# Edge counts from 16 buckets with one product per block, in a graph attention and mixture-of-experts kernel

## The chip, the cores and the metric

One core of one Trainium2 chip runs the whole program. The metric is the device time of one execution in microseconds; lower is better.

## The reference, cut to what matters

Two layers on 1024 nodes with 512 features. The first is a graph attention in which a pair of nodes counts only where an edge joins them, then a mixture of 8 experts (2 chosen per token); the second sums the rows of the neighbours, edge by edge, and then has an 8-head attention and a second mixture.

```python
src = concatenate([_s, _d, arange(1024)])        # 8192 + 8192 + 1024 = 17408 edges
dst = concatenate([_d, _s, arange(1024)])
# layer 0
q, k, v = x @ Wq + bq, x @ Wk + bk, x @ Wv + bv
adj = zeros((N, N)).at[src, dst].set(1.0)
a = q @ k.T / sqrt(512)
a = a * adj + (1.0 - adj) * -1e6
attn = softmax(a, axis=-1) @ v
# layer 1
neigh = segment_sum(feat[src], dst, num_segments=N)
rst = (1.0 + eps[0]) * feat + neigh
```

The kernel needs the matrix of edge counts C[src, dst], 1024 x 1024: `min(C, 1)` is the mask of the first attention, and C itself multiplies the features in the second layer.

## The kernel before, in words

Five engines run hand-written instruction lists and meet at semaphores. Every large product is done in three passes (`three_pass`, line 324): each float operand is split into a high half (made by ScalarE, `copy`) and a low half (made by VectorE, `lo`), and hi x hi, hi x lo and lo x hi are added up in PSUM.

Order of the first part of the program:

1. VectorE sorts the edges (lines 1028 to 1064). Edges lie as 128 partitions x 136 columns (`EC`). Each edge gets its row tile (`src >> 7`, 8 tiles of 128 rows), a running count within the tile, and from two small products on TensorE (line 1610) a place, so that the edges of one tile fill blocks of 128 edges. There are `EDGE_BLOCKS` = 136 + 8 = 144 blocks.
2. TensorE transposes the normalised rows and makes the projections Q and K, eight steps `i` of 24 products (line 1630), then V, eight tiles `t` of 12 (line 1645), then the scores QK, eight tiles of 24 (line 1657). Between them it moves the edges to their places, in 34 groups of four columns of edges (`move_edges`, line 1615): each is eight small products of a lane one-hot (`edge_lanes`, VectorE, `lanes`, line 1077) and a step function (`edge_steps`, ScalarE, `steps`, line 672), added up in PSUM bank 7. Both operands have two buffers: group q of lanes can be written once group q - 2 is moved. A group of moves is placed after the odd `k` of a step.
3. VectorE reads bank 7, subtracts neighbours, and so has for each block and lane the row and the column of its edge (`block_rc`). It builds the row masks (`count_rows`, line 1117), one 128 x 128 per block, the block's tile number (`block_tile`), and adds the values' bias to X.
4. The count loop (lines 1129 and 1678) runs in two rounds, one for each half of the 1024 columns. In a round each of 144 blocks needs a column mask (128 x 512, `lane's column == column number`) and one product, row mask x column mask, added to the PSUM bank of the block's tile (eight tiles, eight banks; the bank comes from a register). Seven of eight column masks are built by VectorE, the eighth by ScalarE as relu(1 - |column - c|). The masks have a ring of 8 groups of four. After a round the eight banks are copied to `CT`, half of them by ScalarE and half by VectorE.
5. The first attention (lines 1189 and 1723) takes tile after tile: mask and maximum on VectorE, exponential on ScalarE, transposes on TensorE, high and low halves, products with V.

SP issues the loads in a fixed order and stores the counts after the second round; GpSimd is idle until the attention's last mask. Two short quotes show the order of the lanes against the moves. On VectorE:

```python
        lanes()
        for i in range(1, 2 * KT):
            projected(i)
            lanes()
            lanes()
```

and on TensorE, in projection `i`:

```python
                if k == KT - 1:
                    got.then_inc(Q0["ps"], 1)
                if i >= 2 and k % 2:
                    move_edges()
```

`projected(i)` makes the low half of projection i, after ScalarE's high half, and the low half of a weight slot.

Of the kernel before, what the change touches and what calls it, by code (L numbers as in the profile page):

```python
# [16 lines left out]
F32 = mybir.dt.float32  # L17
# [16 lines left out]
def build(nc, a, out, ctx):  # L34
# [22 lines left out]
    assert EC % 4 == 0 and HB == 2 and GB == 8 and NT == 8 and KT == 4  # L57
# [52 lines left out]
    edge_lane = edge_const("edge_lane", [EC], F32, 1728)  # L110
    edge_step = edge_const("edge_step", [EC], F32, 2272)
    block_rc = edge_const("block_rc", [2, EDGE_BLOCKS], F32, 0)
    block_f = edge_const("block_f", [EDGE_BLOCKS], F32, 1152)
    minus_column = edge_const("minus_column", [EDGE_BLOCKS], F32, 1728)
    block_tile = edge_const("block_tile", [EDGE_BLOCKS], I32, 2816)
    tile_blocks, tile_end, tile_base = (edge_const(n, [NT], F32, 3392 + 32 * k) for k, n in enumerate(("tile_blocks", "tile_end", "tile_base")))
    tile_i = edge_const("tile_i", [NT], I32, 3488)
    tile_count16 = edge_const("tile_count16", [NT], F16, 3520)
# [61 lines left out]
    in_tile = arena("in_tile", [P, NT, EC], F32, 118)  # L180
    seen_in = arena("seen_in", [P, 1 + NT * EC], F32, 122.5)
    tile_past = arena("tile_past", [P, EDGE_BLOCKS, NT], F32, 128)
# [4 lines left out]
    late_columns = arena("late_columns", [P, RING - 2, 4, HALF], F16, 64)  # L187
    act_columns = arena("act_columns", [P, 4, HALF], F16, 88)
    distance = arena("distance", [P, 2, HALF], F16, 92)
# [83 lines left out]
    act_columned, distanced = sem("act_columned"), sem("distanced")  # L273
    counted_act, counted_dve = sem("counted_act"), sem("counted_dve")
# [63 lines left out]
    def _(sp):  # L338
# [73 lines left out]
        wait(columns_used, 2 * COUNT_GROUPS)  # L412
        for t in range(NT):
            wait((counted_act, counted_dve)[t % 2], NT // 2 + t // 2 + 1)
            sp.dma_start(counts_d[t * P:(t + 1) * P, :], CT[:, t, :]).then_inc(A["stored"], 16)
# [14 lines left out]
        wait(Q0["bias"], 1)  # L430
# [72 lines left out]
    def _(gp):  # L503
# [78 lines left out]

        wait(A["m2"], NT)
# [55 lines left out]
    def _(act):  # L639
# [32 lines left out]
        def steps():  # L672
            q = stepped[0]
            stepped[0] += 1
            if q == 0:
                act.wait_ge(sort_dve, SORTS[1])
            if q >= 2:
                act.wait_ge(edges_moved, q - 1)
            for j in range(4):
                got = act.activation(edge_steps[:, q % 2, j, 0:STEPS_OF], blocks16[:, :], ACT.Sign,  # L680
                                     bias=edge_step[:, 4 * q + j:4 * q + j + 1])
            got.then_inc(edges_stepped, 1)

        for i in range(2 * KT):
# [6 lines left out]
            if i:  # L691
                steps()
            steps()
# [5 lines left out]
        for t in range(NT):  # L699
            act.wait_ge(Q0["s_ps"], t + 1)  # L700
            copy(SR[:, t, :], banks((4, 0)[t % 2]), Q0["s_done"], scale=-D ** -0.5)
            for _ in range(min(2, QUADS - stepped[0])):
                steps()
        assert stepped[0] == QUADS

        per_round = COUNT_GROUPS // 2

        def column_distance(i):

            r, b = i // per_round, 8 * (i % per_round) + 7  # L710
            if i >= 2:
                act.wait_ge(act_columned, i - 1)
            act.activation(distance[:, i % 2, :], columns16[:, r * HALF:(r + 1) * HALF], ACT.Abs,
                           bias=minus_column[:, b:b + 1]).then_inc(distanced, 1)

        def column(i):
            if i >= 4:
                act.wait_ge(columns_used, 2 * (i - 4) + 2)
            act.wait_ge(distanced, i + 1)
            act.activation(act_columns[:, i % 4, :], distance[:, i % 2, :], ACT.Relu, bias=1.0, scale=-1.0).then_inc(act_columned, 1)  # L720

        def counts_out(r):
            act.wait_ge(columns_used, COUNT_GROUPS * (r + 1))
            for t in range(0, NT, 2):
                copy(CT[:, t, r * HALF:(r + 1) * HALF], PS[:, t, :], counted_act)

        act.wait_ge(sort_dve, SORTS[1] + 3)
        column_distance(0)
        for i in range(2 * per_round):
            if i + 1 < 2 * per_round:  # L730
                column_distance(i + 1)
            column(i)
            if i == per_round + 1:
                counts_out(0)
        counts_out(1)

        def no_edge(half, par):
            t = 2 * half + par
            act.wait_ge((counted_act, counted_dve)[par], NT // 2 + half + 1)
# [23 lines left out]
        no_edge(0, 0)  # L763
        no_edge(0, 1)
# [208 lines left out]
    def _(v):  # L973
# [48 lines left out]
        def sort(ins):  # L1022
# [7 lines left out]
        per_tile = [P, NT, EC]  # L1030
        sort(v.tensor_scalar(tile_of[:, :], src_i[:, :], 7, None, ALU.logical_shift_right))
        sort(v.tensor_copy(tile_f[:, :], tile_of[:, :]))
        sort(v.tensor_tensor(in_tile[:, :, :], tile_f[:, :].unsqueeze(1).to_broadcast(per_tile),
                             blocks16[:, 0:NT].unsqueeze(2).to_broadcast(per_tile), ALU.is_equal))
        in_flat = in_tile[:, :, :].rearrange("p t c -> p (t c)")
        sort(v.tensor_tensor_scan(seen_in[:, 1:1 + NT * EC], in_flat, in_flat, 0.0, ALU.add, ALU.max))
        seen_before = seen_in[:, 0:NT * EC].rearrange("p (t c) -> p t c", t=NT)
        seen = seen_in[:, 1:1 + NT * EC].rearrange("p (t c) -> p t c", t=NT)
        v.tensor_tensor(tile_count16[:, :], seen[:, :, EC - 1], seen_before[:, :, 0], ALU.subtract).then_inc(sort_dve, 1)
        sorts[0] += 1  # L1040
        COUNTED = sorts[0]
        assert COUNTED == SORTS[0]

# [9 lines left out]
        v.wait_ge(sort_ps, 1)  # L1053
        tile_rank, tile_total = PS[:, 6, 0:NT], PS[:, 6, NT:2 * NT]
        sort(v.tensor_scalar(tile_i[:, :], tile_total, P - 1.0, None, ALU.add))
        sort(v.tensor_scalar(tile_i[:, :], tile_i[:, :], 7, None, ALU.logical_shift_right))
        sort(v.tensor_copy(tile_blocks[:, :], tile_i[:, :]))
        sort(v.tensor_tensor_scan(tile_end[:, :], ones16[:, 0:NT], tile_blocks[:, :], 0.0, ALU.mult, ALU.add))
        sort(v.tensor_tensor(tile_base[:, :], tile_end[:, :], tile_blocks[:, :], ALU.subtract))
        sort(v.scalar_tensor_tensor(out=tile_base[:, :], in0=tile_base[:, :], scalar=float(P), in1=tile_rank, op0=ALU.mult, op1=ALU.add))  # L1060
        sort(v.tensor_tensor(tile_base[:, :], tile_base[:, :], seen_before[:, :, 0], ALU.subtract))
        sort(v.tensor_tensor(seen, seen, tile_base[:, :].unsqueeze(2).to_broadcast(per_tile), ALU.add))
        sort(v.tensor_tensor(in_tile[:, :, :], in_tile[:, :, :], seen, ALU.mult))
        sort(v.tensor_reduce(out=place_f[:, :], in_=in_tile[:, :, :].rearrange("p t c -> p c t"), axis=X_AXIS, op=ALU.add))
# [26 lines left out]
        sort(v.tensor_scalar(place_i[:, :], place_f[:, :], -1.0, None, ALU.add))  # L1091
        sort(v.tensor_scalar(place_i[:, :], place_i[:, :], 7, None, ALU.logical_shift_right))
        sort(v.tensor_copy(edge_block[:, :], place_i[:, :]))
        sort(v.scalar_tensor_tensor(out=edge_lane[:, :], in0=edge_block[:, :], scalar=-float(P), in1=place_f[:, :], op0=ALU.mult, op1=ALU.add))
        sort(v.tensor_scalar(edge_vals[:, :, 0], src_i[:, :], 1.0, 0.5, ALU.add, ALU.mult))
        sort(v.scalar_tensor_tensor(out=edge_vals[:, :, 0], in0=tile_f[:, :], scalar=-0.5 * P, in1=edge_vals[:, :, 0], op0=ALU.mult, op1=ALU.add))
        sort(v.tensor_scalar(edge_vals[:, :, 1], dst_i[:, :], 0.5, None, ALU.mult))
        sort(v.tensor_scalar(edge_step[:, :], edge_block[:, :], -1.0, -0.5, ALU.mult, ALU.add))
        assert sorts[0] == SORTS[1], sorts
# [15 lines left out]
        sort(v.tensor_scalar(minus_column[:, :], block_rc[:, 1, :], -1.0, None, ALU.mult))  # L1115
# [4 lines left out]
        per_block = [P, EDGE_BLOCKS, NT]  # L1120
        sort(v.tensor_tensor(tile_past[:, :, :], tile_end[:, :].unsqueeze(1).to_broadcast(per_block),
                             blocks16[:, 0:EDGE_BLOCKS].unsqueeze(2).to_broadcast(per_block), ALU.is_le))
        sort(v.tensor_reduce(out=block_f[:, :], in_=tile_past[:, :, :], axis=X_AXIS, op=ALU.add))
        sort(v.tensor_scalar(block_tile[:, :], block_f[:, :], NT - 1.0, None, ALU.min))
# [945 lines left out]
```

## Time and profile before

| | us |
|---|---|
| median of 3 runs | 1089.34 (1089.09 to 1094.71) |
| the profiled execution, its own time | 1087.22 |
| its span, first to last instruction | 1085.4 |
| TensorE busy (matmuls) | 881.8 |
| VectorE busy | 757.5 |
| ScalarE busy | 507.2 |
| GpSimd busy | 357.7 |
| mean granted TensorE clock | 0.916 of 2.4 GHz |

The time of an execution is a little longer than its span, since it holds what lies around the first and the last instruction. Matmuls are pipelined, so TensorE's busy time is an upper view of its work. In the rows, L12 is line 12 of the kernel; `out<-in` names the tiles; a bracket at the end of a row says how long the engine had stood idle before it and what released it.

### The profile page before, as it was taken

How to read it: one execution, taken by the hardware profiler on the slowest of the kernel's cores; microseconds unless marked ns; L12 is line 12 of the kernel's file. 1: busy time of each engine (PE TensorE's matmuls, PEld its weight loads, DVE VectorE, ACT ScalarE, POOL GpSimd, SP SyncE). 2: the span in 40 equal slices, each digit the busy share in tenths (PEclk: the TensorE clock that was granted, in tenths of full speed). 3: DMA queues.
4: the chain of work that ended last, by engine and by line, in shares of the span. 5: the costliest groups of instructions: out<-in, count | busy, mean ns of one | idle time of the engine just before them, and what ended most of it. 6: DMA issues, size and time to landing. Idle time of an engine off the chain costs nothing.

```text
span 1085.4 us, 13783 instructions
## 1 busy us (share of the span) xinstructions
PE 881.8 (81%) x4522; PEld 674.3 (62%) x4522; DVE 757.5 (70%) x1550; ACT 507.2 (47%) x880; POOL 357.7 (33%) x236
## 2 busy tenths in 40 slices
PE   2999997888864999298898788999999987745990
PEld 2777773336743887077687676777777766534860
DVE  8878599886796443857122776778687877796638
ACT  3567517655652554132303046656565656643530
POOL 1000000000202553007321327686786666703520
PEclk9999999998995999589999889999999999966995
DMA  5010000007261444423111330010010050272432
GB/s 160 30 22 2 1 1 1 1 21 265 66 231 59 137 154 139 164 98 98 49 49 29 107 78 1 20 49 20 11 30 20 1 175 1 87 251 100 154 141 103
DMA packets 55523, 84.74 MB, mean 78 GB/s; under 512 B 8976, under 2 KB 31760, under 8 KB 54944
## 3 DMA queue, kind: packets, MB, share of 16 engines
q1 hardware_dynamic: 49376, 63.94, 18.7%
q0 software_dynamic: 6080, 19.93, 5.6%
q8 instruction: 39, 0.64, 0.2%
q14 instruction: 28, 0.23, 0.1%
HBM read 57.11 MB, written 22.54 MB: 73 GB/s over the span
## 4 chain that ended last, share of the span: by engine, by line
PE 57%; DVE 32%; ACT 4%; issue 3%; DMA 2%; POOL 1%; SPq 0%; DVEq 0%; ACTq 0%; POOLq 0%
PE PS L328 37%; DVE late_columns L1138 4%; DVE neg_max L1507 3%; PE PS L1934 3%; PE PS L1949 3%; DVE APL L976 3%; PE PS L1948 2%; PE PS L1923 2%; DVE count_rows L1118 2%; PE PS L1842 2%; PE PS L1623 2%; PE PS L1785 2%; DVE early_columns L1138 1%; DVE XN L1009 1%; DVE XN L1575 1%
## 5 line engine op out<-in xcount | busy, mean ns | idle before, releaser
L615 POOL TENSOR_SCALAR AP__201<-AP__201,rden 128x1024 f32<-128x1024 f32 x64 | 181.9, 2847 | 84.6 <-DVE rden L1512 83.9
L556 POOL TENSOR_TENSOR W1L<-W1R,W1H 128x1024 fp32r<-128x1024 f32 x8 | 18.9, 2390 | 292.0 <-DVE neg_max L1157 288.2
L647 ACT ACTIVATE APH<-PS 128x512 fp32r<-128x512 f32 x128 | 71.7, 597 | 68.7 <-PE PS L1934 44.1
L1507 DVE TENSOR_REDUCE neg_max<-PS 128x1 f32<-128x1024 f32 x64 | 78.2, 1222 | 34.8 <-PE PS L1923 34.0
L976 DVE TENSOR_TENSOR APL<-PS,APH 128x512 fp32r<-128x512 f32 x128 | 83.1, 680 | 24.8 <-ACT APH L647 24.6
L328 PE MATMUL PS<-XTH,WH 128*128 128x512 f32 x224 | 81.8, 412 | 4.5 <-DVE XTL L976 4.5
L1934 PE MATMUL PS<-ident,AP__201 128*128 128x128 f32 x512 | 70.7, 280 | 12.6 <-DVE APL L976 10.8
L328 PE MATMUL PS<-XTL,WH 128*128 128x512 f32 x224 | 78.4, 397 | 0.0
L328 PE MATMUL PS<-XTH,WL 128*128 128x512 f32 x224 | 78.1, 395 | 0.0
L1934 PEld LDWEIGHTS PS<-ident,AP__201 128*128 128x128 f32 x512 | 59.4, 143 | 28.8 <-issue 16.8
L547 POOL CAST WH<-RAW 128x512 fp32r<-128x512 f32 x30 | 23.4, 781 | 158.5 <-PE PS L328 93.5
L917 ACT ACTIVATE AP__201<-PS,neg_max 128x1024 f32<-128x1024 f32 x64 | 71.5, 1117 | 7.4 <-DVE neg_max L1507 6.7
L566 POOL DMA_INDIRECT BX<-normalised,gather_i x38 | 40.1, 1055 | 90.1 <-DVE scatter_i L1329 69.8
L1085 DVE SCALAR_TENSOR_TENSOR edge_lanes<-lanes,edge_lane,edge_vals 128x256 f16<-128x256 f16 x136 | 55.6, 480 | 8.2 <-PE PS L1623 8.2
L1949 PE MATMUL PS<-APH,AV 128*128 128x512 f32 x128 | 50.8, 397 | 11.1 <-DVE APL L976 11.1
L579 POOL DMA_INDIRECT expert_rows<-BY,scatter_i x38 | 37.4, 985 | 61.9 <-ACT BY L647 61.9
L1602 PE MATMUL PS<-ident,XN 128*128 128x128 f32 x128 | 28.3, 398 | 36.2 <-DVE XN L1009 15.7
L680 ACT ACTIVATE edge_steps<-blocks,edge_step 128x145 f16<-128x145 f16 x136 | 45.3, 408 | 20.7 <-PE PS L1623 17.1
L976 DVE TENSOR_TENSOR BHL<-PS,BHH 128x256 fp32r<-128x256 f32 x38 | 16.1, 425 | 51.2 <-ACT BHH L647 51.2
L1138 DVE TENSOR_SCALAR late_columns<-columns,block_rc 128x512 f16<-128x512 f16 x189 | 50.5, 355 | 0.0
L328 PEld LDWEIGHTS PS<-XTH,WH 128*128 128x128 f32 x224 | 42.2, 193 | 13.4 <-POOL WL L549 3.5
L1697 PE MATMUL PS<-late_columns,count_rows 128*128 128x512 f16 x189 | 46.8, 389 | 4.5 <-DVE late_columns L1138 2.5
(302 smaller groups left out, 2393.4 us busy)
## 6 DMA issues: line engine op xcount, KB each, us to landing
YT<-expert_rows SPq DMA_DIRECT2D x12, 512.0 KB, 6.8
counts<-CT SPq DMA_DIRECT2D x8, 512.0 KB, 4.9
W1R<-in_L_ffn_w SPq DMA_DIRECT2D x8, 512.0 KB, 3.9
W2R<-in_L_ffn_w SPq DMA_DIRECT2D x8, 512.0 KB, 5.6
normalised<-XN SPq DMA_DIRECT2D x2, 2048.0 KB, 8.7
CG<-counts SPq DMA_DIRECT2D x8, 512.0 KB, 3.4
RAW<-in_L_gnn_W SPq DMA_DIRECT2D x16, 256.0 KB, 2.8
W1R<-in_L_ffn_W SPq DMA_DIRECT2D x8, 512.0 KB, 8.7
```

What stands on the lines that cost most here:

```text
L328: got = pe.matmul(o, lhs, r, start=first and j == 0, stop=last and j == 2)
L615: gp.tensor_scalar(AP_[:, i % 4, :], AP_[:, i % 4, :], rden[:, i % 4:i % 4 + 1], None, ALU.mult).then_inc(B["norm"], 1)
L647: act.activation(dst, src, Copy, **kw).then_inc(s, 1)
L680: got = act.activation(edge_steps[:, q % 2, j, 0:STEPS_OF], blocks16[:, :], ACT.Sign, bias=edge_step[:, 4 * q + j:4 * q + j + 1])
L917: act.activation(AP_[:, i % 4, :], banks(2 * (i % 2)), ACT.Exp, bias=neg_max[:, i % 4:i % 4 + 1], accum_out=denom[:, i % 4:i % 4 + 1]).the ...
L976: v.tensor_tensor(dst, src, f(hi), ALU.subtract).then_inc(s, 1)
L1085: got = v.scalar_tensor_tensor(out=edge_lanes[:, q % 2, j, :, :], in0=lanes1[:, :].unsqueeze(1).to_broadcast([P, 2, P]), scalar=edge_lane[ ...
L1138: got = v.tensor_scalar(count_columns(k, j), columns16[:, r * HALF:(r + 1) * HALF], block_rc[:, 1, b:b + 1], None, ALU.is_equal)
L1507: v.tensor_reduce(out=neg_max[:, i % 4:i % 4 + 1], in_=banks(2 * (i % 2)), axis=X_AXIS, op=ALU.max, negate=True).then_inc(B["mx"], 1)
L1697: got = pe.matmul(PS[:, ds(held[b % 24]), :].rearrange("p a n -> p (a n)"), count_rows[:, b, :], moving, start=False, stop=False, skip_gro ...
L1934: got = pe.transpose(PS[:, 4 + half, k * P:(k + 1) * P], AP_[:, i % 4, c * P:(c + 1) * P], ident[:, :])
L1949: got = pe.matmul(PS[:, 6, :], AV[:, hp % 2, h, k, :], APH[:, k, :], start=k == 0, stop=k == NT - 1)
```

## The change

Edges are sorted into 16 buckets instead of 8: the row tile times two, plus the half of the columns that the edge's `dst` lies in. There are 136 + 16 = 152 blocks, and each block belongs to one bucket, so it needs one column mask (of 512 columns) and one product: 152 of each, in one round. VectorE makes all column masks, in a ring of 6 groups. Bucket k is summed in PSUM bank k % 8. Banks are handed over by engines that read bucket ends from memory: SP counts finished buckets (`bucket_done`), ScalarE copies a finished bank to `CT` and zeroes it (`bank_free`), GpSimd grants banks to pairs of groups (`banks_granted`), and TensorE waits for the grants. The block-to-bank table comes from a third small product in place of a comparison of all blocks with all tile ends. The operations of the sort are spread between the projections' low halves. The edge products begin in projection 4 in place of 2, and up to four stand in a score tile in place of two. The bias of the values is added tile by tile inside the attention, and the exponential's table is loaded ahead of it.

The core of the diff:

```diff
-    EDGE_BLOCKS = EC + NT
+    BUCKETS = 2 * NT
+    EDGE_BLOCKS = EC + BUCKETS
-    RING = 8
-    SORTS = (5, 23)
+    RING = 6
+    SORTS = (7, 18, 29)
...
     SP:
-        wait(columns_used, 2 * COUNT_GROUPS)
+        wait(sort_dve, PLACED)
+        for k in range(BUCKETS - 1):
+            last = sp.value_load(last_group[0:1, k:k + 1], min_val=1, max_val=COUNT_GROUPS)
+            wait(columns_used, last)
+            sp.sem_inc(bucket_done, 1)
+        wait(columns_used, COUNT_GROUPS)
...
     GpSimd:
+        for g in range(COUNT_GROUPS // 2):
+            needed = gp.value_load(banks_needed[0:1, g:g + 1], min_val=1, max_val=BUCKETS)
+            wait(bank_free, needed)
+            gp.sem_inc(banks_granted, 1)
...
     ScalarE, after the high half of projection i:
-            if i:
+            if i >= 4:
                 steps()
-            steps()
+            if i >= 3:
+                steps()
...
+        def count_out(k):
+
+            if k < BUCKETS - 1:
+                act.wait_ge(bucket_done, k + 1)
+            else:
+                act.wait_ge(columns_used, COUNT_GROUPS)
+            copy(CT[:, k // 2, k % 2 * HALF:(k % 2 + 1) * HALF], PS[:, k % 8, :], counted)
+            if k < 8:
+                act.wait_ge(counted, k + 1)
+                copy(PS[:, k, :], PS[:, k, :], bank_free, scale=0.0)
...
     VectorE:
-        lanes()
-        for i in range(1, 2 * KT):
+        bucket_bases()
+        projected(1)
+        places()
+        projected(2)
+        edge_columns()
+        projected(3)
+        lanes()
+        for i in range(4, 2 * KT):
             projected(i)
+            if i == 5:
+                banks_of_blocks()
             lanes()
             lanes()
...
-        for r in range(2):
-            for g in range(COUNT_GROUPS):
-                k = COUNT_GROUPS * r + g
-                for j in range(4 - g % 2):
...
+        for k in range(COUNT_GROUPS):
+            if k >= RING:
+                v.wait_ge(columns_used, k - RING + 1)
+            elif k == 2:
+                v.wait_ge(Q0["s_ps"], NT)
+            for j in range(4):
+                b = 4 * k + j
+                got = v.tensor_scalar(count_columns(k, j), columns16[:, 0:HALF], block_rc[:, 1, b:b + 1], None, ALU.is_equal)
+            got.then_inc(columns_ready, 1)
...
         mask(0, 0)
         mask(0, 1)
+        value_bias(0)
         p_lo(0, 0)
         for i in range(NT // 2 - 1):
             mask(i + 1, 0)
+            value_bias(2 * i + 1)
             p_lo(i, 1)
             residual(i, 0)
             mask(i + 1, 1)
+            value_bias(2 * i + 2)
             p_lo(i + 1, 0)
...
     TensorE, in projection i:
-                if i >= 2 and k % 2:
+                if i >= 4 and k % 2:
                     move_edges()
...
     TensorE, in score tile t:
-                if k % 2 and moved[0] < QUADS:
+                if moved[0] < QUADS:
                     move_edges()
...
+        for g in range(COUNT_GROUPS):
+            if g % 6 == 0:
+                n = min(24, EDGE_BLOCKS - 4 * g)
+                pe.load(tiles[0:n], block_bank[0:1, 4 * g:4 * g + n])
+                held = [pe.snap(q, min_val=0, max_val=7) for q in tiles[0:n]]
+            if g % 2 == 0:
+                pe.wait_ge(banks_granted, g // 2 + 1)
+            pe.wait_ge(columns_ready, g + 1)
+            for j in range(4):
+                b = 4 * g + j
+                got = pe.matmul(PS[:, ds(held[b % 24]), :].rearrange("p a n -> p (a n)"), count_rows[:, b, :],
+                                count_columns(g, j), start=False, stop=False, skip_group_check=True)
+            got.then_inc(columns_used, 1)
```

`bucket_bases`, `places`, `edge_columns` and `banks_of_blocks` hold the operations of the sort, now over 16 buckets: 11, 2, 9 and 6 of them.

## Rows read from the trace of the kernel before

**Rows 1.** The page, part 1: span, and busy time of TensorE.

```profile
span 1085.4 us, 13783 instructions
PE 881.8 (81%) x4522; PEld 674.3 (62%) x4522; DVE 757.5 (70%) x1550; ACT 507.2 (47%) x880; POOL 357.7 (33%) x236
```

**Rows 2.** Chain of waits, first 300 us: start, length, what.

```profile
135.93 23.53 DVE count_rows L1118 x144
...
168.81 5.51 DVE late_columns L1138 x21
```

**Rows 3.** Windows: stretch, length, busy time by engine, clock, DMA share, GB/s.

```profile
84.90:114.50 29.60, 29.60 (x216) 22.97 (x214) 28.52 (x67) 24.23 (x68) 0.00 (x0) 1.00 0.00 1
163.10:241.40 78.30, 69.67 (x304) 29.95 (x304) 72.51 (x258) 49.63 (x77) 0.00 (x0) 0.98 0.00 1
```

**Rows 4.** Timeline of VectorE in the sort: start, length, instruction, idle time before it.

```profile
5.67 2.43 DVE L1036 TENSOR_TENSOR_SCAN seen_in<-in_tile 128x1088 f32<-128x1088 f32 x1
...
28.98 1.29 DVE L1062 TENSOR_TENSOR seen_in<-seen_in,tile_base 128x1088 f32<-128x1088 f32 x1
...
31.64 2.25 DVE L1064 TENSOR_REDUCE place_f<-in_tile 128x136 f32<-128x1088 f32 x1
```

**Rows 5.** Timeline of all engines around a projection's end, 51 to 55 us.

```profile
51.66 1.11 ACT L688 ACTIVATE KH<-PS,bk 128x1024 fp32r<-128x1024 f32 x1 [1.47 <-PE PS L328]
...
52.80 1.28 DVE L979 SCALAR_TENSOR_TENSOR KL<-PS,bk,KH 128x1024 fp32r<-128x1024 f32 x1 [1.59 <-ACT KH L688]
...
54.60 3.25 DVE L1085 SCALAR_TENSOR_TENSOR edge_lanes<-lanes,edge_lane,edge_vals 128x256 f16<-128x256 f16 x8
```

**Rows 6.** Timeline of all engines in a value tile, 90 to 92 us.

```profile
90.56 0.60 ACT L647 ACTIVATE VH<-PS 128x512 fp32r<-128x512 f32 x1
...
91.19 0.69 DVE L976 TENSOR_TENSOR VL<-PS,VH 128x512 fp32r<-128x512 f32 x1
...
91.80 3.25 DVE L1085 SCALAR_TENSOR_TENSOR edge_lanes<-lanes,edge_lane,edge_vals 128x256 f16<-128x256 f16 x8
```

**Rows 7.** Timeline of TensorE at its waits.

```profile
81.49 0.79 PE L328 MATMUL PS<-WH,XTH 128*128 128x512 f32 x1 [2.59 <-DVE WL L976]
...
84.96 0.47 PE L328 MATMUL PS<-WH,XTH 128*128 128x512 f32 x1
...
86.92 0.48 PE L328 MATMUL PS<-WH,XTH 128*128 128x512 f32 x1
...
168.17 1.68 PE L1697 MATMUL PS<-early_columns,count_rows 128*128 128x512 f16 x7 [3.15 <-DVE early_columns L1138]
...
175.45 1.68 PE L1697 MATMUL PS<-late_columns,count_rows 128*128 128x512 f16 x7 [1.72 <-DVE early_columns L1138]
...
207.91 3.16 PE L1697 MATMUL PS<-late_columns,count_rows 128*128 128x512 f16 x7 [2.02 <-DVE late_columns L1138]
```

**Rows 8.** Windows of 3 us behind three of those waits.

```profile
81.50:84.50 3.00, 3.00 (x9) 2.09 (x10) 1.52 (x4) 0.00 (x0) 0.00 (x0) 0.50 0.02 5
168.20:171.20 3.00, 3.00 (x14) 1.41 (x15) 3.00 (x13) 2.14 (x4) 0.00 (x0) 1.00 0.00 0
208.00:211.00 3.00, 3.00 (x8) 1.12 (x9) 3.00 (x13) 0.17 (x1) 0.00 (x0) 0.50 0.00 0
```

**Rows 9.** Timeline from the last edge product to the first column mask.

```profile
134.67 0.46 DVE L1113 COPY block_sum<-PS 128x290 f32<-128x290 f32 x1 [5.02 <-PE PS L1623]
...
161.96 1.02 ACT L647 ACTIVATE SR<-PS 128x1024 f32<-128x1024 f32 x1 [4.41 <-PE PS L328]
...
162.42 4.43 DVE L1126 TENSOR_TENSOR X<-X,row 128x4096 f32<-128x4096 f32 x1
```

**Rows 10.** Timeline from the first mask of scores to the first value product.

```profile
243.78 1.22 DVE L1153 SCALAR_TENSOR_TENSOR SM<-CT,SR 128x1024 f32<-128x1024 f32 x1
...
252.52 0.50 PE L328 MATMUL PS<-VH,PTH 128*128 128x512 f32 x1 [0.55 <-DVE PTL L976]
```

More of the change, by code:

```diff
@@ L272, in build @@
     rows_ready, columns_ready, columns_used = sem("rows_ready"), sem("columns_ready"), sem("columns_used")
-    act_columned, distanced = sem("act_columned"), sem("distanced")
-    counted_act, counted_dve = sem("counted_act"), sem("counted_dve")
+    bank_free, banks_granted, bucket_done = sem("bank_free"), sem("banks_granted"), sem("bucket_done")
+    counted = sem("counted")
     raw_in = [sem(f"raw_in{s}") for s in range(4)]
@@ L409, in results @@
                                  y_d[c * N + 2 * g * P:c * N + (2 * g + 2) * P, :].rearrange("(t p) d -> p t d", p=P)).then_inc(M["y_in"][g], 16)
-        wait(columns_used, 2 * COUNT_GROUPS)
+        wait(sort_dve, PLACED)
[4 more added lines that the diff above has]
+        wait(columns_used, COUNT_GROUPS)
         for t in range(NT):
-            wait((counted_act, counted_dve)[t % 2], NT // 2 + t // 2 + 1)
+            wait(counted, 2 * t + 2)
             sp.dma_start(counts_d[t * P:(t + 1) * P, :], CT[:, t, :]).then_inc(A["stored"], 16)
@@ L429, in _ @@
         results(0)
-        wait(Q0["bias"], 1)
+        wait(Q0["bias"], NT)
         sp.dma_start(row0[:, :], a["L1_gnn_b2"].partition_broadcast(P)).then_inc(row0_in, 16)
@@ L699, in _ @@
         for t in range(NT):
+            for _ in range(min(4, QUADS - stepped[0])):
+                steps()
             act.wait_ge(Q0["s_ps"], t + 1)
             copy(SR[:, t, :], banks((4, 0)[t % 2]), Q0["s_done"], scale=-D ** -0.5)
-            for _ in range(min(2, QUADS - stepped[0])):
-                steps()
         assert stepped[0] == QUADS
[L706 to L735, printed above, removed]
+        def count_out(k):
[7 more added lines that the diff above has]
+                copy(PS[:, k, :], PS[:, k, :], bank_free, scale=0.0)
         def no_edge(half, par):
             t = 2 * half + par
-            act.wait_ge((counted_act, counted_dve)[par], NT // 2 + half + 1)
+            act.wait_ge(counted, 2 * t + 2)
             if t >= 2:
@@ L761, in w1_hi @@
             copy(W1H[which][:, e, :, :], W1R[:, e, :, :], M["w_hi"])
-        no_edge(0, 0)
-        no_edge(0, 1)
+        for k in range(BUCKETS):
+            count_out(k)
+            if k in (1, 3):
+                no_edge(0, k // 2)
+            if k == BUCKETS - 2:
+                act.activation(inv[:, 0:1], neg_col[:, 0:1], ACT.Exp, scale=-1.0)
         softmax(0, 0)
@@ L1060, in _ @@
[L1060 to L1064, printed above, removed]
+        in_flat = in_bucket[:, :, :].rearrange("p t c -> p (t c)")
@@ new lines, in _, with bucket_bases @@
+        sort(v.tensor_tensor_scan(seen_in[:, 1:1 + BUCKETS * EC], in_flat, in_flat, 0.0, ALU.add, ALU.max))
+        seen_before = seen_in[:, 0:BUCKETS * EC].rearrange("p (t c) -> p t c", t=BUCKETS)
+        seen = seen_in[:, 1:1 + BUCKETS * EC].rearrange("p (t c) -> p t c", t=BUCKETS)
+        sort(v.tensor_tensor(bucket_count16[:, :], seen[:, :, EC - 1], seen_before[:, :, 0], ALU.subtract))
+        assert sorts[0] == SORTS[0]
+        def bucket_bases():
+            v.wait_ge(sort_ps, 1)
+            rank, total = PS[:, 6, 0:BUCKETS], PS[:, 6, BUCKETS:2 * BUCKETS]
+            sort(v.tensor_scalar(bucket_i[:, :], total, P - 1.0, None, ALU.add))
+            sort(v.tensor_scalar(bucket_i[:, :], bucket_i[:, :], 7, None, ALU.logical_shift_right))
+            sort(v.tensor_scalar(bucket_blocks[:, :], bucket_i[:, :], 1.0, None, ALU.max))
+            sort(v.tensor_tensor_scan(bucket_end[:, :], ones16[:, 0:BUCKETS], bucket_blocks[:, :], 0.0, ALU.mult, ALU.add))
+            sort(v.tensor_tensor(bucket_base[:, :], bucket_end[:, :], bucket_blocks[:, :], ALU.subtract))
+            sort(v.scalar_tensor_tensor(out=bucket_base[:, :], in0=bucket_base[:, :], scalar=float(P), in1=rank, op0=ALU.mult, op1=ALU.add))
+            sort(v.tensor_tensor(bucket_base[:, :], bucket_base[:, :], seen_before[:, :, 0], ALU.subtract))
+            sort(v.tensor_tensor(seen, seen, bucket_base[:, :].unsqueeze(2).to_broadcast(per_bucket), ALU.add))
+            sort(v.tensor_tensor(end_mask[0:BUCKETS, :], bucket_end[0:BUCKETS, :], ident[0:BUCKETS, 0:BUCKETS], ALU.mult))
+            sort(v.tensor_reduce(out=end_col[0:BUCKETS, :], in_=end_mask[0:BUCKETS, :], axis=X_AXIS, op=ALU.add))
+            sort(v.tensor_scalar(past16[0:BUCKETS, :], blocks16[0:BUCKETS, 0:EDGE_BLOCKS], end_col[0:BUCKETS, :], None, ALU.is_ge))
+            assert sorts[0] == SORTS[1], sorts
@@ new lines, in places, with edge_columns @@
+        def places():
+            sort(v.tensor_tensor(in_bucket[:, :, :], in_bucket[:, :, :], seen, ALU.mult))
+            sort(v.tensor_reduce(out=place_f[:, :], in_=in_bucket[:, :, :].rearrange("p t c -> p c t"), axis=X_AXIS, op=ALU.add))
+        def edge_columns():
+            sort(v.tensor_scalar(place_i[:, :], place_f[:, :], -1.0, None, ALU.add))
+            sort(v.tensor_scalar(place_i[:, :], place_i[:, :], 7, None, ALU.logical_shift_right))
+            sort(v.tensor_copy(edge_block[:, :], place_i[:, :]))
+            sort(v.scalar_tensor_tensor(out=edge_lane[:, :], in0=edge_block[:, :], scalar=-float(P), in1=place_f[:, :], op0=ALU.mult, op1=ALU.add))
+            sort(v.tensor_scalar(edge_vals[:, :, 0], src_i[:, :], 1.0, 0.5, ALU.add, ALU.mult))
+            sort(v.scalar_tensor_tensor(out=edge_vals[:, :, 0], in0=tile_f[:, :], scalar=-0.5 * P, in1=edge_vals[:, :, 0], op0=ALU.mult, op1=ALU.add))
+            sort(v.tensor_scalar(dst_i[:, :], dst_i[:, :], HALF - 1, None, ALU.bitwise_and))
+            sort(v.tensor_scalar(edge_vals[:, :, 1], dst_i[:, :], 0.5, None, ALU.mult))
+            sort(v.tensor_scalar(edge_step[:, :], edge_block[:, :], -1.0, -0.5, ALU.mult, ALU.add))
+            assert sorts[0] == SORTS[2], sorts
@@ L1119, in _, with value_bias @@
         got.then_inc(rows_ready, 1)
[L1120 to L1124, printed above, removed]
-        v.wait_ge(row0_in, 16)
-        v.tensor_tensor(X[:, :, :], X[:, :, :], row0[:, :].unsqueeze(1).to_broadcast([P, NT, D]), ALU.add).then_inc(Q0["bias"], 1)
-        v.wait_ge(Q0["bias"], 1)
-        for r in range(2):
-            for g in range(COUNT_GROUPS):
-                k = COUNT_GROUPS * r + g
-                if k >= RING:
-                    v.wait_ge(columns_used, k - RING + 1)
-                elif k == 2:
-                    v.wait_ge(Q0["s_ps"], NT)
-                for j in range(4 - g % 2):
-                    b = 4 * g + j
-                    got = v.tensor_scalar(count_columns(k, j), columns16[:, r * HALF:(r + 1) * HALF],
-                                          block_rc[:, 1, b:b + 1], None, ALU.is_equal)
-                got.then_inc(columns_ready, 1)
-            v.wait_ge(columns_used, COUNT_GROUPS * (r + 1))
-            for t in range(1, NT, 2):
-                v.tensor_copy(CT[:, t, r * HALF:(r + 1) * HALF], PS[:, t, :]).then_inc(counted_dve, 1)
+        for k in range(COUNT_GROUPS):
[7 more added lines that the diff above has]
+            got.then_inc(columns_ready, 1)
+        v.wait_ge(row0_in, 16)
+        def value_bias(t):
+            v.tensor_tensor(X[:, t, :], X[:, t, :], row0[:, :], ALU.add).then_inc(Q0["bias"], 1)
         def mask(half, par):
             t = 2 * half + par
-            v.wait_ge((counted_act, counted_dve)[par], NT // 2 + half + 1)
+            v.wait_ge(counted, 2 * t + 2)
             v.wait_ge(Q0["s_done"], NT)
@@ L1172, in residual @@
             v.wait_ge(A["rden"], t + 1)
+            v.wait_ge(Q0["bias"], t + 1)
             x = X[:, ds(t), :].rearrange("p a n -> p (a n)")
@@ L1608, in _ @@
         pe.wait_ge(setup, 12)
-        pe.wait_ge(sort_dve, SORTS[0])
-        pe.matmul(PS[:, 6, 0:NT], before16[:, :], tile_count16[:, :], start=True, stop=True)
-        pe.matmul(PS[:, 6, NT:2 * NT], ones16[:, :], tile_count16[:, :], start=True, stop=True).then_inc(sort_ps, 1)
         moved = [0]
@@ L1638, in _ @@
                     got.then_inc(Q0["ps"], 1)
-                if i >= 2 and k % 2:
+                if i >= 4 and k % 2:
                     move_edges()
+            if i == 0:
+                pe.wait_ge(sort_dve, SORTS[0])
+                pe.matmul(PS[:, 6, 0:BUCKETS], before16[:, :], bucket_count16[:, :], start=True, stop=True)
+                pe.matmul(PS[:, 6, BUCKETS:2 * BUCKETS], ones16[:, :], bucket_count16[:, :], start=True, stop=True).then_inc(sort_ps, 1)
+            elif i == 3:
+                pe.wait_ge(sort_dve, SORTS[1])
+                pe.matmul(PS[:, 6, 2 * BUCKETS:2 * BUCKETS + EDGE_BLOCKS], ones16[0:BUCKETS, :], past16[0:BUCKETS, :],
+                          start=True, stop=True).then_inc(sort_ps, 1)
         pe.wait_ge(w_ready, 12)
@@ L1721, in values @@
             got.then_inc(A["av_ps"], 1)
-        pe.wait_ge(counted_act, NT)
-        pe.wait_ge(counted_dve, NT)
+        pe.wait_ge(counted, BUCKETS)
         p_transposes(0, 0)
```

105 lines of the change are left out of this document (38 added, 67 removed).

## The prediction

> **What bounds the kernel now.** I read the page first: 1085.4 us of span, TensorE busy for 881.8 us of it [rows 1]. Next comes the chain of waits, cut to the first 300 us, because the change touches nothing later. It has two kinds of stretches. Where the projections run, it follows TensorE; from the last edge product on it follows VectorE, through 23.53 us of row masks and then the column masks [rows 2]. The windows say the same: while the values are projected TensorE is busy for 29.60 of 29.60 us, but VectorE for 28.52 as well; in the count loop TensorE is busy for 69.67 of 78.3 us and VectorE for 72.51 [rows 3]. So the count loop is paid in VectorE instructions, and the stage ahead of it has no slack on either engine. The change takes work out of the first and re-times the second.
>
> **The loop that gets shorter.** A block of edges now belongs to one bucket of (row tile, half of columns), so it needs one column mask and one product, where it had two. Before, VectorE made 252 masks and ScalarE 36; after, VectorE makes all 152. One costs 5.51 / 21 = 0.262 us on VectorE's path [rows 2]. After the last edge product VectorE copies sums (about 1 us) and makes 152 row masks at 23.53 / 144 = 0.163 us, 24.8 us; the two operations that compared blocks with tile ends and the 4.43 us bias addition [rows 9] are gone from there. In the new order half a score tile and five more follow the last edge product, 2.7 + 5 x 5.44 (4.41 + 1.03, the spacing of the score copies [rows 9]) = 29.9 us, so row masks and the first two groups of columns (8 x 0.262 = 2.1 us) hide behind them. The third group writes over the keys' low halves and waits for the end of the scores, which I call S (162.0 us before: the last copy starts at 161.96 [rows 9]).
>
> After S: 144 masks x 0.262 = 37.8 us on VectorE. TensorE waits 1.1 us for the last score copy, zeroes 8 banks (about 1.9 us) and then needs at most 4 x 1.68 / 7 = 0.96 us per group [rows 7] against VectorE's 1.05, so VectorE sets the pace. Then the mask of tile 0, its exponential, transposes, and high and low halves: before, 252.52 - 243.78 = 8.7 us [rows 10], 0.5 of it a table load that is now made early, so 8.3. First value product at S + 46.2; before, at S + 90.5 (252.52 - 162.0). **The loop gives 44.3 us back.**
>
> Work I cost at nothing: 16 copies of banks (0.6 us each) and 8 zeroings on ScalarE, some 15 us beside 38 us in which it has nothing else; the eight bias additions, 4.43 / 8 = 0.55 us each [rows 9], which lie where VectorE waits over 2 us for ScalarE's exponential in each attention tile. SP's and POOL's register reads and waits (15 and 19) are not shown by any row. The nearest row is TensorE's read of 24 registers, ahead of which it stood 1.72 us [rows 7]. A bucket lasts 9 blocks x 0.262 = 2.4 us, and bank k is wanted again only when bucket k + 8 begins, about 7 buckets or 17 us after bucket k ended, so anything below 15 us stays hidden. Bounds: 0 and, if TensorE's seven register reads are paid in full, 7 x 1.7 = 12 us; I take 0, since the same reads already run in the loop before, where VectorE still sets the pace.
>
> **The stage that gets longer.** (a) Sorting over 16 buckets doubles the [128 x 1088] operations: 1.29 us, scan 2.43, reduction 2.25 [rows 4]. The scan moves behind the first transposes, so the start gains 0.7 us. (b) From there VectorE's order is: scan and count (5 us), low half 0, bases (4.6), low half 1, places (2.45 + 4.45), low half 2, edge columns (2.5), low half 3, first lanes. TensorE starts at 27.0, has no edge products in the first four projections and ends them at about 48.9; the fifth needs low half 2, which VectorE ends at 50.3: a stall of 1.4 us. Its first edge product needs the first lanes, ready at 57.0, when TensorE has been waiting since 53.1: 3.9 us.
>
> (c) The important one is an order. Before, VectorE made three groups of lanes before the first projection that has edge products inside, so TensorE's next group was always there. Now it makes one, then in turn per projection: low half, weights' low half, two groups of lanes. I counted: when TensorE reaches the end of projection i (i = 4 to 7), the edge product placed there is number 2i - 6, and VectorE has made 2i - 7; the missing one stands behind low half i, which waits for ScalarE's copy of this very projection. So TensorE waits for the whole round: from the end of the product to lanes ready is 0.06 + 1.14 (ScalarE, 51.66 to 52.80) + 1.80 (two low halves, 52.80 to 54.60) + 1.67 (half of the eight lanes of 3.25) = 4.7 us [rows 5]. Before, that product started 0.16 us ahead of that end: +4.86 us, four times, 19.4 us, and 1.4 us more in the sixth, where six small operations stand ahead of the lanes.
>
> (d) The same lag goes through the values, since both sides advance by two per tile: ScalarE 0.63 (90.56 to 91.19), low half 0.61, lanes 1.67, 2.96 us of waiting [rows 6]. TensorE's own work in a tile is a little under two groups of 1.96 us (84.96 to 86.92 [rows 7]), 3.84 us; with 0.16 us of tail and the wait the period is 6.96 us, against 3.92 before (91.19 to the next low half, 0.61 + 3.25 and the gaps), +3.04, eight times: 24.3 us. (e) The old wait at 81.49 (2.59 us) and the half clock behind it (1.5 us) vanish into this, -4.1. The 34 edge groups are the same number, ten now among the scores in place of six. At full clock S moves by -0.7 + 1.4 + 3.9 + 19.4 + 1.4 + 24.3 - 4.1 = **+45.6 us**.
>
> **The clock.** These stalls also decide TensorE's clock. After the 2.59 us wait at 81.49 it runs at 0.50 of full, 1.2 GHz, and so it does after the 2.02 us wait at 207.91; after 3.15 us at 168.17 it stays at 1.00, 2.4 GHz [rows 7, 8]. At 81.49 the group of six products and eight small ones takes 3.47 us (to 84.96), the next one 1.96 (to 86.92) [rows 7]: a fall costs 1.5 us, on TensorE, which is on the path here. There are 13 stalls of 2.9 us or more. Bounds: none falls, 0; the clock stays low for all the work between them (32 us in the values, 27 in the projections), +59. The rows say two of three; as these stalls return every 7 to 11.5 us, I take 12 of 13: **+18 us**.
>
> [...]
>
> **Sum.** -44.3 + 45.6 + 18 = +19.3 us. The profiled execution took 1087.22 us, so 1106.5 by its own time; the median of the runs shown is 1089.34, 2.1 above, and the predicted median is 1108.5 us.
>
> **Rivals.** (1) The stalls come as counted, but the clock mostly stays up, as at 168.17: 0 to 6 us in place of 18, 1.3 to 7 us in all, 1090 to 1097. For it: the waits in the values are shorter than the one at 168.17. Against: a shorter one fell. Chance 0.14. (2) Faster: TensorE does not wait at the second edge product of each group, since the lanes are there, so that (c), (d) and the clock go and only -0.7 + 1.4 + 3.9 + 1.4 - 4.1 = 1.9 stays: -42 us, 1047. For it: no such wait is in the trace of before, where lanes are two ahead of the products. Against: the count, which has no slack. It decides from the point where twelve stalls, clock included, cost less than 3.5 us each; I have 5.1. Chance 0.11, with anything between. (3) The count loop is bound by something else than VectorE, bank grants or register reads on TensorE: +12 us on my forecast, 1120, up to 1130. Against: the slack of 15 us. Chance 0.12. (4) The change does not halve the loop, because padding fills the blocks: against it stands the fixed count of 152. No chance of its own.
>
> **Numbers.** The forecast itself has 0.63, with its own range 1100 to 1118 (8 to 13 falls, a few us in the sorting). Leaving out two tenths: 1088 to 1124. A measurement of this kernel tells 0.5%, 5.4 us, from no change. Faster: rival 2, 0.12 with the edge of rival 1. Same: most of rival 1, 0.08. Slower: 0.80.
>
> **What would show it.** In the profile after: TensorE idle for about 4.7 us, released by VectorE's lanes, ahead of the edge products that end projections 5 to 8, and about 3 us ahead of one in each value tile; a granted clock under 1.00 from 50 to 175 us; scores ending between 220 and 228 us; column masks without a gap for 38 us; value products 46 us after the scores. It is wrong if edge products after each tile start without idle time, or if the column masks wait for products.

## The result, and the profile after

The changed kernel takes 1117.89 us (median of 4 runs, 1116.22 to 1119.48) against 1090.2 us for the kernel before, measured together with it: ratio 1.0254, 95% interval 1.0218 to 1.029. It is slower by about 28 us. The forecast was 1108.5 us, slower, with a range of 1088 to 1124. The profiled execution took 1118.83 us, 31.6 more than the profiled one of before; the differences of traces below are against that.

| | before | after |
|---|---|---|
| scores end (S) | 162.0 us | 234.8 us |
| first mask of scores | 243.8 us | 273.4 us |
| first value product | 252.5 us | 281.8 us |
| span | 1085.4 us | 1117.0 us |
| mean granted clock | 0.916 | 0.892 |

So S came 72.8 us later, the count loop gave 43.5 us back (252.5 - 162.0 = 90.5 became 281.8 - 234.8 = 47.0), and 2.3 us more were lost between there and the end of the kernel.

The page of the changed kernel, part 1, answers to [rows 1]. TensorE and VectorE are both less busy than before, in a longer span.

```profile
span 1117.0 us, 13327 instructions
PE 876.7 (78%) x4379; PEld 680.8 (61%) x4379; DVE 735.6 (66%) x1465; ACT 469.6 (42%) x825; POOL 358.1 (32%) x236
```

The windows of the changed kernel answer to the first of [rows 3]; the columns are the same (the last three are clock, DMA share, GB/s). From 110 to 180 us, the values, TensorE is busy for 47.89 of 70 us (the stage of the values had no idle time before, 29.60 of 29.60 us [rows 3]), VectorE for 29.27, and the clock is 0.74.

```profile
50.00:110.00 60.00, 35.84 (x156) 27.36 (x154) 27.07 (x59) 19.31 (x46) 0.00 (x0) 0.82 0.08 14
110.00:180.00 70.00, 47.89 (x224) 36.28 (x224) 29.27 (x69) 22.24 (x65) 0.00 (x0) 0.74 0.00 1
180.00:215.00 35.00, 32.41 (x194) 25.75 (x195) 28.96 (x104) 18.90 (x49) 0.00 (x0) 0.95 0.00 1
```

With both engines idle in the same stretch the question is who waits for whom. The timeline of TensorE has all of it: first the wait for the low half at 51.81, then the first edge group, then the last edge group of each of four projections, then of the value tiles (three of the eight are shown, the others read 2.99 or 3.00 as well). The second column is how long the edge group takes: 1.15 to 1.21 us where TensorE starts at half clock, 0.71 us at full clock, as at 138.34.

```profile
51.81 0.70 PE L332 MATMUL PS<-XTH,WH 128*128 128x512 f32 x2 [1.13 <-DVE QL L979]
58.24 1.21 PE L1646 MATMUL PS<-edge_steps,edge_lanes 128*128 128x153 f16 x8 [3.43 <-DVE edge_lanes L1119]
67.76 1.15 PE L1646 MATMUL PS<-edge_steps,edge_lanes 128*128 128x153 f16 x8 [4.71 <-DVE edge_lanes L1119]
...
82.44 1.21 PE L1646 MATMUL PS<-edge_steps,edge_lanes 128*128 128x153 f16 x8 [6.24 <-DVE edge_lanes L1119]
...
96.74 1.21 PE L1646 MATMUL PS<-edge_steps,edge_lanes 128*128 128x153 f16 x8 [4.71 <-DVE edge_lanes L1119]
...
110.76 1.21 PE L1646 MATMUL PS<-edge_steps,edge_lanes 128*128 128x153 f16 x8 [4.71 <-DVE edge_lanes L1119]
...
120.15 1.21 PE L1646 MATMUL PS<-edge_steps,edge_lanes 128*128 128x153 f16 x8 [2.99 <-DVE edge_lanes L1119]
...
129.93 1.21 PE L1646 MATMUL PS<-edge_steps,edge_lanes 128*128 128x153 f16 x8 [3.00 <-DVE edge_lanes L1119]
...
138.34 0.71 PE L1646 MATMUL PS<-edge_steps,edge_lanes 128*128 128x153 f16 x8 [2.99 <-DVE edge_lanes L1119]
```

The chain of waits shows the round itself: TensorE's products end at 117.17, then come ScalarE's high half, VectorE's low half, four lanes, and only then the edge group, which at half clock takes 1.21 us. It is the pattern of [rows 6], with TensorE now waiting at its end.

```profile
115.66 1.51 PE PS L332 x6
117.17 0.02 issue
117.20 0.60 ACT VH L662
117.80 0.02 issue
117.83 0.69 DVE VL L976
118.52 1.59 DVE edge_lanes L1119 x4
120.11 0.04 issue
120.15 1.21 PE PS L1646 x8
```

In the count loop the timeline shows VectorE setting the pace, as [rows 2] had it. TensorE waits once for 0.85 us, which the profile puts down to GpSimd's grant of banks, and this holds up VectorE's ring for 0.68 us; from there on the masks stand without a gap until the first mask of scores at 273.38.

```profile
238.70 1.90 PE L1720 MATMUL PS<-early_columns,count_rows 128*128 128x512 f16 x8 [0.85 <-POOLq L517]
...
239.77 2.19 DVE L1160 TENSOR_SCALAR early_columns<-columns,block_rc 128x512 f16<-128x512 f16 x8 [0.68 <-PE PS L1720]
...
271.28 2.19 DVE L1160 TENSOR_SCALAR early_columns<-columns,block_rc 128x512 f16<-128x512 f16 x8
273.38 1.23 DVE L1174 SCALAR_TENSOR_TENSOR SM<-CT,SR 128x1024 f32<-128x1024 f32 x1
```

### The profile page after: what moved, and what is told of

Its sections match the earlier page's. It is cut to its first block, busy times and chain, and to the rows that moved or that the text cites. A ratio compares the mean times of both kernels' runs of the same rounds, so it can differ in the third digit from the quotient of the medians.

```text
span 1117.0 us, 13327 instructions
## 1 busy us (share of the span) xinstructions
PE 876.7 (78%) x4379; PEld 680.8 (61%) x4379; DVE 735.6 (66%) x1465; ACT 469.6 (42%) x825; POOL 358.1 (32%) x236
## 4 chain that ended last, share of the span: by engine, by line
PE 56%; DVE 32%; ACT 5%; issue 4%; DMA 1%; POOL 1%; DVEq 0%; POOLq 0%; SPq 0%; ACTq 0%
PE PS L332 37%; DVE neg_max L1533 3%; PE PS L1955 3%; PE PS L1970 3%; DVE APL L976 3%; PE PS L1646 3%; PE PS L1969 2%; PE PS L1944 2%; PE PS L1863 2%; DVE late_columns L1160 2%; DVE edge_lanes L1119 2%; PE PS L1806 2%; DVE XN L1009 1%; DVE early_columns L1160 1%; DVE stats L984 1%
## 5 line engine op out<-in xcount | busy, mean ns | idle before, releaser
L332 PE MATMUL PS<-XTH,WH 128*128 128x512 f32 x224 | 85.2, 429 | 5.6 <-DVE XTL L976 4.5
L332 PE MATMUL PS<-XTL,WH 128*128 128x512 f32 x224 | 81.2, 411 | 0.0
L1646 PE MATMUL PS<-edge_steps,edge_lanes 128*128 128x153 f16 x272 | 32.4, 279 | 47.7 <-DVE edge_lanes L1119 47.7
L1646 PEld LDWEIGHTS PS<-edge_steps,edge_lanes 128*128 128x128 f16 x272 | 24.0, 119 | 60.6 <-DVE edge_lanes L1119 53.6
L332 PEld LDWEIGHTS PS<-XTH,WH 128*128 128x128 f32 x224 | 44.5, 204 | 15.3 <-POOL WL L558 3.5
L1628 PEld LDWEIGHTS PS<-ident,XN 128*128 128x128 f32 x128 | 23.0, 207 | 49.3 <-issue 24.6
L332 PEld LDWEIGHTS PS<-XTL,WH 128*128 128x128 f32 x224 | 45.3, 202 | 9.5
```

What stands on the lines that cost most here:

```text
L332: got = pe.matmul(o, lhs, r, start=first and j == 0, stop=last and j == 2)
L1628: got = pe.transpose(PS[:, t % 4, k * P:(k + 1) * P], src[:, t, k * P:(k + 1) * P], ident[:, :])
L1646: got = pe.matmul(PS[:, 7, n * STEPS_OF:(n + 1) * STEPS_OF], edge_lanes[:, q % 2, j, n, :], edge_steps[:, q % 2, j, 0:STEPS_OF], start=c = ...
```

## The experiments

Theory A is that of the prediction: the lanes lag one group behind, so that TensorE waits a whole round twelve times and its clock falls after the waits. Theory B: VectorE is crowded by the longer sort, and the order of the lanes does not matter. The first four kernels below were measured against a median of 1088.37 us for the kernel before, the last two against 1089.82 us.

**A lead of two.**

```diff
         projected(3)
         lanes()
+        lanes()
+        lanes()
...
-            if i >= 4:
-                steps()
-            if i >= 3:
-                steps()
+            for _ in range(3 if i == 3 else 2 if i > 3 else 0):
+                steps()
```

> The changed kernel with the old lead given back: VectorE makes three groups of lanes (and ScalarE three of steps) behind the fourth projection in place of one, and two per step from there as before. Theory A (TensorE waits a whole round, product to high half to low half to lanes, at the end of each of four projections and eight value tiles, and its clock falls behind these waits): the twelve waits of 4.7 and 3.0 us are gone, 44 us, and with them most of the clock's loss of about 27 us; 1047 us (1040 to 1056), scores ending some 65 to 70 us earlier than 234.7. Theory B (the stage is long because the sort over 16 buckets and its operations crowd VectorE, and the waits would come up elsewhere): above 1100 us.

Measured: 1056.2 us, ratio to the kernel before 0.9691 (0.9663 to 0.9719). Theory B is out: the order alone, with no instruction less, takes 62 us away and turns the change into a gain of 3%. S comes at 171.1 us, 63.7 earlier than in the changed kernel. The number expected was 9 us too low. The timeline of TensorE says what stayed: from 30 us to the end of the scores its only waits are three, and two of them are long enough to matter, one for the first lanes and one at the start of the values, which is the old wait of 2.59 us [rows 7] come back.

```profile
51.70 0.70 PE L332 MATMUL PS<-XTH,WH 128*128 128x512 f32 x2 [1.13 <-DVE QL L977]
58.13 1.21 PE L1646 MATMUL PS<-edge_steps,edge_lanes 128*128 128x153 f16 x8 [3.43 <-DVE edge_lanes L1117]
87.61 0.52 PE L332 MATMUL PS<-WH,XTH 128*128 128x512 f32 x1 [2.56 <-DVE WL L974]
```

The windows after these two waits, with the projections between them, give a clock of 0.52 and 0.67, with 1.00 in the middle. The expectation had taken away nearly the whole of the clock's loss; 6.10 us at 0.52 and 5.20 us at 0.67 are still a loss of 2.9 and 1.7 us (length times what the clock lacks to 1.00).

```profile
58.20:64.30 6.10, 6.10 (x21) 4.74 (x22) 3.04 (x8) 1.36 (x4) 0.00 (x0) 0.52 0.55 70
64.40:85.00 20.60, 20.60 (x128) 16.36 (x126) 16.48 (x36) 13.23 (x31) 0.00 (x0) 1.00 0.00 1
87.60:92.80 5.20, 5.19 (x22) 3.90 (x23) 2.98 (x8) 1.37 (x4) 0.00 (x0) 0.67 0.00 0
```

**A lead of one.** Two `lanes()` behind `projected(3)` and two `steps()` from `i >= 3`, in place of three and three.

> As the first kernel of this series, with only one more group of lanes and of steps (two behind the fourth projection). Theory A: the group for a tile's end is there, but the next one comes a round later: short waits of about 1.5 us in the projections and 1.2 us in the values, too short to bring the clock down, so 14 us over the kernel with a lead of two: 1061 us (1054 to 1070). Theory B: above 1100 us. If a lead of one were enough, it equals the kernel with a lead of two.

Measured: 1070.22 us, ratio 0.9818 (0.9788 to 0.9849), 14.0 us over the lead of two, which is the difference expected; the number itself, 1061, was again 9 us too low, just outside its range. The timeline of TensorE shows the short waits: 1.35 and 1.37 us in the projections (2.88 where the six small operations stand ahead of the lanes) and 1.0 us eight times in the values. They add up to 13.7 us, so next to nothing of the 14 us is left for the clock.

```profile
68.54 0.71 PE L1645 MATMUL PS<-edge_steps,edge_lanes 128*128 128x153 f16 x8 [1.35 <-DVE edge_lanes L1117]
78.29 0.71 PE L1645 MATMUL PS<-edge_steps,edge_lanes 128*128 128x153 f16 x8 [2.88 <-DVE edge_lanes L1117]
...
108.10 0.71 PE L1645 MATMUL PS<-edge_steps,edge_lanes 128*128 128x153 f16 x8 [1.01 <-DVE edge_lanes L1117]
```

**The waits filled.** All waits stay, TensorE works through them on a bank that nobody reads. This takes the clock out of the cost and leaves the rest (in the trace 0.37 to 0.39 us of each wait stay unfilled, 1.91 of the longest).

```diff
+        def fill(n):
+            for _ in range(n):
+                pe.matmul(PS[:, 5, :], ones16[:, :], columns16[:, 0:HALF], start=True, stop=True)
...
                 if i >= 4 and k % 2:
+                    fill(20 if k == 3 else 14 if i == 4 else 0)
                     move_edges()
...
                 if k % 2:
+                    fill(12 if k == 3 else 0)
                     move_edges()
```

> The changed kernel with every wait left where it is, but TensorE fills it: 20 products of 512 columns ahead of each projection's last edge group, 14 ahead of the first one, 12 ahead of each value tile's last edge group, written to a bank that nobody reads. Theory A with the clock as a cost of its own: the clock stays at 1.00 in the values and the time falls by 20 to 27 us, to 1091 to 1098. If the clock's fall costs nothing on this path: 1118 or more.

Measured: 1094.72 us, as expected, ratio 1.0044 (1.0025 to 1.0063). Against 1117.89, the clock alone costs some 23 us, which are saved here by giving TensorE 190 products for nothing. The windows of this kernel over the projections and the values read 1.00, where the changed kernel had 0.82 and 0.74; S comes at 211.0 us in place of 234.8.

```profile
50.00:104.00 54.00, 49.43 (x261) 31.05 (x260) 29.15 (x63) 19.54 (x46) 0.00 (x0) 1.00 0.09 16
104.00:160.00 56.00, 53.20 (x312) 32.64 (x311) 29.76 (x70) 24.32 (x71) 0.00 (x0) 1.00 0.00 1
```

**The old kernel with the lag.** The mirror: only the lead is taken from the kernel before.

```diff
         lanes()
-        for i in range(1, 2 * KT):
+        projected(1)
+        for i in range(2, 2 * KT):
             projected(i)
             lanes()
             lanes()
...
-            if i:
-                steps()
-            steps()
+            for _ in range((1, 0)[i] if i < 2 else 2):
+                steps()
```

> The kernel before, with its lead taken away and nothing else changed: one group of lanes and steps behind the first projection in place of three. Theory A: waits of 4.7 us at the end of six projections and 3.0 us at the end of eight value tiles appear, 29 + 24 us, and about 2 us of clock with each, 14 x 2 = 28: 1170 us (1150 to 1180). Theory B: within 10 us of 1090.

Measured: 1172.29 us, ratio 1.0758 (1.0727 to 1.0788), as expected: +84 us for an order of the same instructions. Its timeline has 4.71 us six times and 3.0 us eight times. The two groups that are no longer made ahead are now made in the scores, and there three waits of 2.4 us stand that had not been expected; the profile names ScalarE's steps as what ended them. So some 7 of the 84 us are waits in the scores and not in the projections and values. From S (245.6) to the first mask of scores it takes 80.8 us, the kernel before 81.8 and all kernels with the new loop 38.6: the loop's gain does not depend on what happens ahead of it.

```profile
64.64 1.15 PE L1623 MATMUL PS<-edge_steps,edge_lanes 128*128 128x145 f16 x8 [4.71 <-DVE edge_lanes L1084]
...
135.30 0.69 PE L1623 MATMUL PS<-edge_steps,edge_lanes 128*128 128x145 f16 x8 [3.00 <-DVE edge_lanes L1084]
...
194.52 0.67 PE L1623 MATMUL PS<-edge_steps,edge_lanes 128*128 128x145 f16 x8 [2.42 <-ACT edge_steps L680]
```

**A later start.** From the lead of two: the edge products begin one projection later, and the first lanes are there when TensorE comes. The edit is shown against the changed kernel.

```diff
-            if i >= 4:
-                steps()
-            if i >= 3:
+            for _ in range((2, 1, 2, 2, 2)[i - 3] if i >= 3 else 0):
                 steps()
...
         projected(3)
         lanes()
-        for i in range(4, 2 * KT):
+        lanes()
+        projected(4)
+        banks_of_blocks()
+        lanes()
+        for i in range(5, 2 * KT):
             projected(i)
-            if i == 5:
-                banks_of_blocks()
             lanes()
             lanes()
...
-                if i >= 4 and k % 2:
+                if i >= 5 and k % 2:
                     move_edges()
```

> The kernel with a lead of two, but the edge products begin one projection later (the sixth), so that the first lanes are there when TensorE comes; the two groups left over move into the scores. If the wait of 3.43 us ahead of the first edge product and the clock behind it are on the path: 1051 us (1048 to 1054) against 1056.2 for a lead of two. If the wait only moves, to the row masks that follow the last edge product: 1056 or more.

Measured: 1046.78 us, ratio 0.9608 (0.958 to 0.9636). The wait of 3.43 us is gone and the clock is 1.00 from 50 to 79 us. S comes at 164.8, 6.3 us earlier than with the lead of two. The gain in time, 9 us, is larger than the 5 expected, and the time lies below the range of 1048 to 1054: 3.1 us of it lie behind the first value product, where no edit was made (836.2 us from there to the end with the lead of two, 833.1 here). That stretch is taken up below.

**The values' start.** On top of that, each wait of the first value tile stands where it is needed. This edit is shown against the later start.

```diff
-        pe.wait_ge(w_ready, 12)
-        for par in range(2):
-            pe.wait_ge(Q0["lo"][par], 4)
+        pe.wait_ge(Q0["lo"][0], 4)
         for t in range(NT):
+            if t == 2:
+                pe.wait_ge(Q0["lo"][1], 4)
...
             for k in range(KT):
+                if t == 0:
+                    pe.wait_ge(w_ready, 9 + k)
```

> As the kernel with the later start, and the first value tile waits for the low half of each weight slot when it uses it, and for the last projection's low half only at its third tile, not for all of it ahead of the first. The wait of 2.56 us at the start of the values goes, and with it a fall of the clock (1.5 us): 4 us less than the later start alone, 1047 us (1044 to 1050). If the values are paced by VectorE anyway, which makes two groups of lanes per tile, 1051, no gain.

Measured: 1042.2 us, ratio 0.9571 (0.9543 to 0.96). The wait of 2.57 us ahead of the values is gone; in its place there is one of 0.62 us for lanes. S comes at 160.2 us, 4.6 earlier than with the later start, and earlier than in the kernel before although TensorE's edge groups are wider. The time is 4.6 us less too, about the 4 expected, but the intervals of the two ratios overlap, so this last step is likely rather than shown. It is the fastest version here, 48 us or 4.3% below the kernel before.

## Why the prediction was right, and which terms were off

- *The loop gives 44.3 us back.* It gave 43.5. VectorE's pace was right: 38.6 us from S to the mask against 37.8, of which 0.68 is the one wait behind TensorE's 0.85. But for it, bank grants, bucket ends, register reads, the copies of banks and the bias additions are hidden, as costed.
- *The sort.* The waits were 1.13 and 3.43 us, forecast 1.4 and 3.9.
- *The lag.* 4.71, 6.24, 4.71 and 4.71 us against 4.7 and one longer by 1.4; eight times 2.99 against 2.96. The kernels with a lead of two and of one, and the mirror in the old kernel, show that the order alone makes them.
- *The clock, the mis-sized term.* I had 12 falls of 1.5 us, 18 us; filling the waits shows about 23 us (S by 23.8), 1.8 for each of 13 waits. The windows of the 13 stretches after the waits agree: all read below 1.00, and length times the missing clock is 1.4 to 3.1 us, 2.0 in the mean. Three of the 13 are shown.

```profile
120.20:126.90 6.70, 6.70 (x28) 5.11 (x28) 1.48 (x4) 0.09 (x1) 0.00 (x0) 0.58 0.00 0
138.30:144.00 5.70, 5.66 (x28) 4.20 (x28) 1.57 (x4) 0.17 (x1) 0.00 (x0) 0.70 0.00 0
164.20:171.00 6.80, 6.80 (x28) 5.22 (x28) 1.47 (x4) 0.08 (x1) 0.00 (x0) 0.55 0.01 2
```

In five of the eight value tiles the clock is still low for the next edge group (1.25 us at 123.81). Behind the one fall that was priced from [rows 7], 1.5 us, that group took 0.94 us (at 84.22): it was among the short falls. The range of 0 to 59 held it.
- *Full clock.* With the clock out of the way (the filled waits) S is at 211.0, where the forecast gives 162.0 + 45.6 = 207.6, 3.4 us too low. 1.4 of them are the value tile, which takes 7.13 us in place of 6.96. The edge group of 153 columns in place of 145 is the smaller part of it: with 145 columns, in the old kernel with the lag, the tile takes 7.07 us, so the width makes 0.06 us a tile and the sum had the tile itself 0.11 too short. The other 2 us are not taken apart.
- *Behind the first value product* 2.3 us were lost that no step spoke of. The eight traces fall into two groups. Where the first value product takes 0.50 us, at full clock (the kernel before, the later start, the values' start), 832.9 to 833.2 us follow it; where it takes 0.79 or 0.80 us (the other five, the old kernel with the lag among them), 834.7 to 836.2. That points at the clock at this place, but no run isolates it.
- *Rival 2* did not come about, since TensorE did wait; the kernel with a lead of two is the one that it describes, and it takes 1056.2 us where the rival had 1047. 4.1 of these 9 us are the old wait at the start of the values with its clock, which the rival had left out together with the lag and which comes back when the lag goes; a further 2.9 are the half clock after the wait of 3.43 us, which it had put at nothing. The mean cost of a lagging step was 5.1 us in the forecast; the decision point of 3.5 us lay between the lead of one (14 / 12 = 1.2) and the changed kernel (62 / 12 = 5.1).
- *The signs.* One of them failed: the scores were to end between 220 and 228 us and ended at 234.8, by the two terms above that were too small. In all, the profiled executions are 31.6 us apart where the sum had 19.3: 0.8 from the loop, 3.4 at full clock, 5.8 from the clock and 2.3 behind the first value product. All four lie on the same side, so no error hid another; 1117.89 is at the upper edge of the inner range, 1100 to 1118.

The section "HAM oscillation — how this bites in real kernels" of the Trainium skill's "TensorE: Matmul & The Clock Gate" describes a loop that waits some 3 to 5 us for a transfer in every iteration and starts each burst of products at half clock. The changed kernel agrees with it in part: all 13 stretches lost clock, but after three of the waits of 3.0 us (138.34, 155.44 and 182.59) the edge group still took 0.71 us, and the clock fell about 1 us later. The old kernel with the lag agrees less, as the last section shows.

## What to carry to other kernels

When an order written by hand is moved, count for each wait which number the consumer asks for and which number the producer has made by then; here a lead cut from two groups to one cost 14 us, and a lead of two cut to a lag of one group 62 us in the new kernel, 84 us in the old, with the same instructions. A producer that stands behind the consumer's own result makes the consumer wait for the whole round, and no busy share of the kernel before showed it. A gain in one stage is best judged by its own start and end (S to the first mask, 81.8 to 38.6 us), so that a loss in another stage does not hide it.

## What the runs showed of the hardware that was not expected

The same wait does not always bring the clock down. In the old kernel with the lag the value tiles wait 3.0 us each time. For the first 24 us the clock reads 0.98 and the tiles follow at 7.07 us (132.34, 139.41, 146.48); then, with the same instructions, it reads 0.80 and they follow at 8.4 to 8.7. In the changed kernel all eight of the same length were followed by a lower clock, five at once and three after about 1 us. So a wait on TensorE cost here its length plus something between 0 us (the first three of 3.0 us in the old kernel with the lag) and 3.1 us (after 164.15 in the changed kernel), which one profile of before could not narrow.

```profile
128.00:152.00 24.00, 14.79 (x100) 10.99 (x101) 13.32 (x32) 9.44 (x29) 0.00 (x0) 0.98 0.00 1
152.00:183.50 31.50, 19.71 (x98) 14.89 (x96) 13.71 (x32) 11.89 (x36) 0.00 (x0) 0.80 0.00 1
```

And work for nothing can pay: the products that fill the waits made the changed kernel 2% faster. Removing the waits is worth more, 5.5%.
